# Layer 1's second head in two quarters: turning rows with VectorE and transfers instead of with TensorE

## The chip, the cores and the metric

The kernel runs on one core of a Trainium2 chip. The metric is the time of one execution in microseconds on the device. Lower is better.

## The reference

Four graph layers act on `x` (4096 x 128) with one adjacency matrix `adj` (4096 x 4096). The change lies in layer 1 (two attention heads) and in the preparation of layer 2's input:

```python
# layer 1, for each head i (K = 2)
h = x_norm @ ff0_w[i].T
e = leaky_relu(s_src[:, None] + s_dst[None, :]);  atten = softmax(where(mask, e, NEG), axis=1)
att = _ln(atten @ h + x, g2, b2)
h_next = h_next + elu(att @ ff1_w[i].T) / K
# between the layers
x = x + h_next
h = maximum(_layernorm(x), 0.0)
# layer 2 begins with
Wh = h @ W;  f_src = Wh @ a[:D];  f_dst = Wh @ a[D:]
```

So after a head's sums are complete there are two more small matrix products for each block of rows: `att @ ff1_w.T`, and, after the second head, `h @ W` for the next layer. For either one, the rows have to be turned (features on the partitions).

## The kernel before

The 4096 rows of the result are worked in four quarters (`Q = 4`) of 1024 (`S = 8` blocks of 128), and each quarter is a run over `T = 32` tiles k. In layer 1 (h = 1 and h = 2 for its two heads) VectorE makes for each tile k one tile of exponentials, 128 x 1024, into one of four slots (`ring`, L1323). TensorE multiplies it into `acc` in two halves of 512 columns (L504, two records of the trace for each half, so four for a tile). VectorE can be at most four tiles ahead, because tile k waits until TensorE has used tile k - 4.

There is no planner. Small work is hung behind fixed tiles by lists `ks`: `run(h, q, at(ks, steps))` runs step j on that engine directly after its tile `ks[j]`. TensorE, VectorE and ScalarE work through their programs in order, and talk by semaphores. During run (2, q) the engines finish quarter q - 1 of the second head (`post1(1, q - 1)`), and prepare that quarter's input of layer 2 (`feed(3, ...)`):

- ScalarE copies `acc` to `U` as soon as the previous run has ended (`wide_take`, L978), TensorE turns the sums back (`sums_back`, L557), VectorE divides, adds the residual from `V`, and takes statistics (L1454, L1127 to L1140). Step `scal` (L1146, L1150) gives scale and shift, and ScalarE writes normalised rows to `V` (L788, signal `n_norm`).
- TensorE turns `V` by eight transposes into `turn` (L519), ScalarE widens `turn` into `U` with scale and bias (L810, `n_wide`), TensorE multiplies by `ff1T` (`apply`, L570), ScalarE takes exp and relu (L1017, L1018), VectorE forms the elu and adds to `X` (L1470, L1482, `post_done`).
- VectorE takes statistics of `X`, ScalarE normalises again into `V` (`f_norm`), TensorE turns `V` (L519), ScalarE widens it to `U` with sums in `hpart` (L808, `f_wide`), VectorE adds those sums (`halves`, L1190), TensorE multiplies by `proj2` (`project`, L542), and ScalarE copies the result to `G` and `score2` (L882, L884, `f_placed`).

In TensorE's and ScalarE's programs the runs (2, 1) and (2, 2) are the two turns of a loop whose q is a register; run (2, 3) is written out. In VectorE's all are written out. With q a register, `fixed(q)` is false. At the head of ScalarE's loop stands a load of the activation table (shown at L978).

The first head turns its rows in another way already: VectorE transposes 32 x 32 blocks from `V` to `U` (L1501, `small_turned`), and `move_blocks` (L275) puts the blocks in place by 16 transfers of 32 KB from `U` back to `V`, eight issued from SP's queue and eight from ScalarE's. ScalarE then waits for `blocks_moved` and widens `V` into `U` (L1011).

`bring_back(q)` in SP's queue (L431) loads the saved input of quarter q into `V` for the residual, when `V` has been read.

Of the kernel before, what the change touches and what calls it, by code (L numbers as in the profile page):

```python
# [64 lines left out]
def graph_layers(nc, x, adj, adj_t, diag, alpha, w0_t, bias0, ff0, ff0_t, ff1_t, attn, g1, b1, g2, b2,  # L65
# [17 lines left out]
    EDGE = (2, 3, 0, 1)  # L83
    EB = len(EDGE)
    SPARE = 2
    WEIGHTS = 15
    WARM = 7

    with ExitStack() as ctx:
# [150 lines left out]
        def fixed(v):  # L240
            return isinstance(v, int)
# [22 lines left out]

        flat_v = V[:, :, :].rearrange("p s d -> p (s d)")

        def move_blocks(eng, q, groups):

            eng.wait_ge(small_turned, q + 1)
            given, taker = (U[:, 0:QC], flat_v) if q < Q else (part_turned, U[:, 0:QC])  # L270
            for i in groups:
                for d in range(4):
                    src = given[32 * i:32 * i + 32, :].rearrange("p (s d r) -> p s d r", d=4, r=32)[:, :, d, :]
                    dst = taker[32 * d:32 * d + 32, :].rearrange("p (s i r) -> p s i r", i=4, r=32)[:, :, i, :]
                    eng.dma_start(dst, src).then_inc(blocks_moved, 16)  # L275
# [8 lines left out]
        def all_summed(h, q):  # L284

            n = q + h * Q
            if h in (1, 2):
                return acc_summed[1], n + 1
            return acc_summed[NB - 1], n + 1 if h == 0 else n + 1 - 2 * Q

        def last_of(q):
            return fixed(q) and q == Q - 1
# [45 lines left out]
        def _(sp):  # L338
# [87 lines left out]
            def bring_back(q):  # L426
                if q == 0:
                    sp.wait_ge(post_done, 2 * Q)
                else:
                    sp.wait_ge(f_turned, q + Q + 1)  # L430
                sp.dma_start(V[:, :, :].rearrange("p s d -> p (s d)"), span(inputs1, q * QC, QC)).then_inc(back, 16)  # L431
            sp.wait_ge(*all_summed(1, Q - 1))
            load_rows(2, 2)
# [1 line left out]
            move_blocks(sp, 3, (0, 1))  # L435
            sp.wait_ge(saved, 16 * Q)
            bring_back(0)
            bring_back(1)
            bring_back(2)
            bring_back(3)  # L440

# [37 lines left out]
        def _(pe):  # L479
# [42 lines left out]
            def feed(h, p, weights, wide, spreads, posts):  # L522

                at = p if h == 0 else Q if h == 1 else p - 2 * Q + 1

                def turned():
                    pe.wait_ge(f_norm, p + 1)
                    wait(pe, rows_kept, spreads)
                    if h == 1:
                        for s in range(S):  # L530
                            mm = pe.transpose(turn[:, s * P:(s + 1) * P], G[:, 1, (p - Q) * S + s, 0:P], ident[:, :])
                    else:
                        mm = turn_v()
                    mm.then_inc(f_turned, 1)

                def project():
                    pe.wait_ge(f_wide, at + 1)
                    wait(pe, f_placed, p if h < 3 else p - Q)
                    wait(pe, post_done, posts)
                    for s in range(S):  # L540
                        dst = mix[:, 0, s * 4:s * 4 + 4] if h == 1 else mix[:, s // 3, (s % 3) * PW:(s % 3) * PW + wide]
                        mm = pe.matmul(dst, U[:, s * P:(s + 1) * P], weights, start=True, stop=True, skip_group_check=True)  # L542
                    mm.then_inc(f_projected, 1)
                return turned, project

            def post1(h, q, spreads, feeds):

                j = q + h * Q

                def sums_back():  # L550
                    pe.wait_ge(acc_taken, taken(1 + h, q) + 2)
                    if h == 0 and fixed(q) and q == 0:
                        pe.wait_ge(bias_made, late_top[2])
                    elif h == 1 and fixed(q) and q == Q - 1:
                        pe.wait_ge(bias_made, early_top[3])
                    for s in range(S):
                        mm = pe.matmul(mix[:, s // 3, (s % 3) * DW:(s % 3) * DW + DW], U[:, s * P:(s + 1) * P], back_w[h],  # L557
                                       start=True, stop=True, skip_group_check=True)
                    mm.then_inc(rows_back, 1)

                def turned():
                    pe.wait_ge(n_norm, j + 1)
                    pe.wait_ge(rows_kept, spreads)
                    turn_v().then_inc(n_turned, 1)

                def apply():
                    pe.wait_ge(n_wide, j + 1)
                    pe.wait_ge(f_placed, feeds)
                    for s in range(S):
                        mm = pe.matmul(mixed[:, s * P:(s + 1) * P], U[:, s * P:(s + 1) * P], ff1T[:, h, :],  # L570
                                       start=True, stop=True, skip_group_check=True)
                    mm.then_inc(ff_done, 1)
                return (sums_back, apply) if h == 0 else (sums_back, turned, apply)

            def spread_top(i):
                pe.wait_ge(top_placed, i)
# [127 lines left out]
            def stage2(q):  # L704
                m = kept_rows[1]
                if fixed(q) and q == 0:
                    ks = [0, 23]
                    run(2, q, at(ks, post1(0, Q - 1, m, 2 * Q)))
                    return
                steps = post1(1, q - 1, m, q - 1 + 2 * Q) + feed(3, q - 1 + 3 * Q, proj2, D + 2, m, q + 2 * Q)  # L710
                if last_of(q):
                    ks = [1, 11, 12, 25, 26, 27, 29]
                    run(2, q, at(ks, steps + (lambda: spread_top(early_top[3]), lambda: spread_rows(m))))
                else:
                    ks = [1, 13, 15, 27, 28]
                    run(2, q, at(ks, steps))
            stage2(0)
            pe.wait_ge(qv2_placed, 1)
# [58 lines left out]
        def _(act):  # L777
# [55 lines left out]
            def feed(h, p, q, between=()):  # L833
# [33 lines left out]
                at = p if h == 0 else Q if h == 1 else p - 2 * Q + 1  # L867
                if h == 3:
                    wait(act, half_summed, 0 if fixed(q) and q == 0 else q * 1)
                    widen(f_turned, at + 1, f_wide, halves=True)  # L870
                else:
                    widen(f_turned, at + 1, f_wide)
                for step in between:
# [114 lines left out]
            def post1(h, q, beside=(), fed=False):  # L988
# [14 lines left out]
                    settle()  # L1003
                normalise(of_v, lambda s: U3[:, s, 0:D], local(scale), local(shift), ACT.Identity, n_norm)
                act.wait_ge(n_norm, j + 1)
                if h == 0:
                    move_blocks(act, q, (2, 3))
                    act.wait_ge(blocks_moved, 256 * (q + 1))
                    for c in range(2):
                        half = slice(c * BANK, (c + 1) * BANK)  # L1010
                        ins = act.activation(U[:, half], flat_v[:, half], ACT.Identity, bias=b2c, scale=g2c)  # L1011
                    ins.then_inc(n_wide, 1)
                else:
                    widen(n_turned, q + 1, n_wide, g2c, b2c)
                ready(ACT.Exp)
                act.wait_ge(ff_done, j + 1)
                act.activation(V[:, :, :], mixed3, ACT.Exp)  # L1017
# [79 lines left out]

            def store(q):
                wide_take(q + 4 * Q)
                move_blocks(act, Q + q, range(4))  # L1100
                act.wait_ge(post_done, q + 4 * Q + 1)
                act.dma_start(span(out.rearrange("(t p) d -> p t d", p=P), q * S, S), V[:, :, :]).then_inc(stored, 16)
            for q in range(Q - 1):
# [9 lines left out]
        def _(dve):  # L1113
# [42 lines left out]
            def feed(h, p, q):  # L1156
# [30 lines left out]
                def halves():  # L1187
                    dve.wait_ge(f_wide, p - 2 * Q + 2)
                    wait(dve, half_summed, 0 if fixed(q) and q == 0 else q * 1)
                    dve.scalar_tensor_tensor(hmean, hpart[0], hpart[1], hmean, ALU.add, ALU.add).then_inc(half_summed, 1)  # L1190
                steps = statistics(lambda s: blocks(X, q, 1, s)[:, 0, :], f_var) + [first_scales]
                if h == 1:
                    half, rest = statistics(of_v, f2_var)
# [1 line left out]
                if h == 1 and not (fixed(p) and p == 2 * Q - 1):  # L1195
                    steps += [lambda c=c: dots(c) for c in range(4)]
                if h == 3:
                    steps += [halves]
                return steps

            def of_v(s):
# [233 lines left out]
            def post1(h, q):  # L1435
# [63 lines left out]
                def small_turns():  # L1499
                    dve.wait_ge(n_norm, j + 1)  # L1500
                    dve.transpose(flat, V[:, :, :].rearrange("p s d -> p (s d)")).then_inc(small_turned, 1)  # L1501
                turns = [small_turns] if h == 0 else []
                steps = [residual, residual_rest] + statistics(lambda s: U3[:, s, 0:D], n_var) + [scal] + turns + [elu, add]
                return steps if h == 0 else steps + [own_pattern, own_pattern_rest]

# [33 lines left out]
            def stage2(q):  # L1539
                steps = post1(1, q - 1) + feed(3, q - 1 + 3 * Q, q - 1)  # L1540
                if last_of(q):
                    ks = [4, 4, 6, 8, 10, 17, 17, 12, 14, 19, 21, 24, 28, 29, 30]
                    run(2, q, at(ks, steps + early_of(3)))
                else:
                    ks = [4, 5, 8, 10, 12, 19, 20, 13, 16, 21, 23, 25, 29]
                    run(2, q, at(ks, steps))
            for q in range(1, Q):
                stage2(q)
# [61 lines left out]
            def post3(q):  # L1610
# [23 lines left out]

                def first_half():
                    st.wait()
                    dve.wait_ge(blocks_moved, 256 * (Q + q + 1))
                    if q > 0:
                        dve.wait_ge(stored, q * 16)
                    st.mark(results(slice(0, HALF)))  # L1640
# [48 lines left out]
```

## Time and profile before

| | us |
|---|---|
| time, median of 3 runs | 1198.27 (1197.99 to 1199.12) |
| time of the profiled execution | 1198.28 |
| its span | 1196.5 |
| TensorE busy in the span | 1191.9 |
| VectorE busy | 936.4 |
| ScalarE busy | 301.6 |

The span runs from the first to the last instruction; the profiled execution's time holds 1.8 us more, which lies around it. Busy time counts matmuls until their modelled end, so it doesn't say that TensorE is at its peak. Granted clock is given as a share of 2.4 GHz, and was 1.00 over the span.

### The profile page before, as it was taken

How to read it: one execution, taken by the hardware profiler on the slowest of the kernel's cores; microseconds unless marked ns; L12 is line 12 of the kernel's file. 1: busy time of each engine (PE TensorE's matmuls, PEld its weight loads, DVE VectorE, ACT ScalarE, POOL GpSimd, SP SyncE). 2: the span in 40 equal slices, each digit the busy share in tenths (PEclk: the TensorE clock that was granted, in tenths of full speed). 3: DMA queues.
4: the chain of work that ended last, by engine and by line, in shares of the span. 5: the costliest groups of instructions: out<-in, count | busy, mean ns of one | idle time of the engine just before them, and what ended most of it. 6: DMA issues, size and time to landing. Idle time of an engine off the chain costs nothing.

```text
span 1196.5 us, 16807 instructions
## 1 busy us (share of the span) xinstructions
PE 1191.9 (100%) x6299; PEld 823.5 (69%) x6299; DVE 936.4 (78%) x1704; ACT 301.6 (25%) x732; POOL 10.4 (1%) x21
## 2 busy tenths in 40 slices
PE   9999999999999999999999999999999999999999
PEld 9999999965444444444544547999999974444455
DVE  5548675798878788878888796798787869887886
ACT  3312122234323232422323134541212121000000
POOL 3000000000000000000000000000000000000000
PEclk9999999999999999999999999999999999999999
DMA  9888888700111102110000000022303068999930
GB/s 318 301 270 289 299 293 302 254 23 10 45 18 36 18 35 35 53 18 18 1 18 0 18 1 19 2 86 109 141 0 141 1 258 305 313 332 319 321 85 18
DMA packets 79284, 153.18 MB, mean 128 GB/s; under 512 B 35456, under 2 KB 44016, under 8 KB 79216
## 3 DMA queue, kind: packets, MB, share of 16 engines
q1 hardware_dynamic: 53264, 145.43, 34.8%
q10 hardware_dynamic: 25456, 6.30, 2.4%
q8 instruction: 43, 0.70, 0.2%
q0 software_dynamic: 496, 0.55, 0.1%
q14 instruction: 25, 0.20, 0.1%
HBM read 144.33 MB, written 4.24 MB: 124 GB/s over the span
## 4 chain that ended last, share of the span: by engine, by line
PE 98%; DVE 1%; ACT 0%; issue 0%; DVEq 0%
PE acc L504 51%; PE acc L488 37%; PE acc L761 4%; PE mix L570 1%; PE mix L557 1%; PE mix L542 1%; PE turn L519 1%; PE acc L769 1%; DVE ring L1323 0%; PE turn L515 0%; PE mix L628 0%; PE mix L515 0%; PE turn L638 0%; DVE U L1454 0%; PE mix L645 0%; PE turn L633 0%
## 5 line engine op out<-in xcount | busy, mean ns | idle before, releaser
L1323 DVE SCALAR_TENSOR_TENSOR ring<-G,score,mask 128x1024 f32<-128x1024 f32 x372 | 464.7, 1279 | 62.8 <-PE acc L504 33.0
L504 PE MATMUL acc<-ring,G 128*128 128x512 f32 x1000 | 436.2, 593 | 0.2 <-DVE acc L1263 0.2
L504 PEld LDWEIGHTS acc<-ring,G 128*128 128x128 f32 x1000 | 186.6, 190 | 226.9 <-issue 209.8
L488 PE MATMUL acc<-G,ring 128*128 128x129 f32 x2240 | 254.3, 275 | 0.1
L488 PEld LDWEIGHTS acc<-G,ring 128*128 128x128 f32 x2240 | 252.1, 192 | 1.4 <-issue 1.1
L488 PE MATMUL acc<-G,mask 128*128 128x129 f32 x1648 | 186.2, 275 | 0.0
L488 PEld LDWEIGHTS acc<-G,mask 128*128 128x128 f32 x1648 | 185.0, 192 | 0.0
L504 PE MATMUL acc<-mask,G 128*128 128x512 f32 x384 | 165.8, 593 | 0.0
L1597 DVE TENSOR_TENSOR ring<-ring,mask 128x1024 f32<-128x1024 f32 x120 | 146.7, 1223 | 11.4 <-DVE ring L1597 0.9
L504 PEld LDWEIGHTS acc<-mask,G 128*128 128x128 f32 x384 | 72.6, 190 | 91.0 <-issue 89.8
L1361 DVE TENSOR_SCALAR mask<-mask 128x1024 uint8<-128x1024 f32 x103 | 68.6, 688 | 38.0 <-DMA mask<-in_adj_t 37.7
L800 ACT ACTIVATE dev<-var 128x8 f32<-128x8 f32 x28 | 5.9, 209 | 233.8 <-DVE var L1140 233.8
L978 ACT COPY U<-acc 128x512 f32<-128x512 f32 x22 | 12.9, 585 | 171.1 <-PE acc L504 171.1
L761 PE MATMUL acc<-mask,G 128*128 128x384 f32 (+1 forms) x128 | 48.6, 540 | 0.0
L986 ACT COPY U<-acc 128x387 f32<-128x387 f32 (+1 forms) x24 | 10.4, 446 | 129.2 <-PE acc L488 128.4
L761 PEld LDWEIGHTS acc<-mask,G 128*128 128x128 f32 x128 | 24.2, 190 | 24.0 <-issue 15.6
L788 ACT ACTIVATE V<-X,shift,scale 128x128 f32<-128x128 f32 (+1 forms) x88 | 35.0, 480 | 0.0
L784 ACT ACT_TABLE_LOAD x26 | 33.4, 1283 | 2.7 <-ACT V L788 1.6
L780 ACT COPY cols<-ident 128x1 f32<-128x1 f32 x40 | 7.6, 190 | 90.2 <-DVE shift L1150 29.1
L788 ACT ACTIVATE V<-U,shift,scale 128x128 f32<-128x128 f32 x64 | 25.5, 480 | 8.8 <-DVE shift L1150 8.8
L1177 DVE SCALAR_TENSOR_TENSOR V<-G,ring 128x128 f32<-128x128 f32 x96 | 21.3, 286 | 5.3 <-ACT G L788 5.2
L488 PE MATMUL acc<-G 128*128 128x129 f32 x160 | 19.6, 276 | 0.3 <-DVE G L1323 0.3
(210 smaller groups left out, 692.6 us busy)
## 6 DMA issues: line engine op xcount, KB each, us to landing
mask<-in_adj SPq DMA_DIRECT2D x128, 512.0 KB, 5.5
mask<-in_adj_t SPq DMA_DIRECT2D x103, 512.0 KB, 4.9
ring<-in_adj_t SPq DMA_DIRECT2D x18, 512.0 KB, 4.9
G<-given_rows SPq DMA_DIRECT2D x10, 512.0 KB, 3.9
G<-in_adj_t SPq DMA_DIRECT2D x4, 512.0 KB, 5.1
inputs<-V ACTq DMA_DIRECT2D x4, 512.0 KB, 2.7
V<-inputs SPq DMA_DIRECT2D x4, 512.0 KB, 3.9
X<-in_x SPq DMA_DIRECT2D x3, 512.0 KB, 9.9
```

Of the source, the lines that this page charges most:

```text
L488: mm = pe.matmul(acc[:, b, (s % 3) * DW:(s % 3) * DW + DW], lhs[:, s * P:(s + 1) * P], g, start=(k == 0 and s % 3 == 0), stop=(k == T - 1) ...
L504: mm = pe.matmul(acc[:, c, :], g, moving[:, c * BANK:(c + 1) * BANK], start=(k == 0), stop=(k == T - 1), skip_group_check=True)
L519: mm = pe.transpose(turn[:, s * P:(s + 1) * P], V[:, s, :], ident[:, :])
L542: mm = pe.matmul(dst, U[:, s * P:(s + 1) * P], weights, start=True, stop=True, skip_group_check=True)
L761: mm = pe.matmul(acc[:, c, 0:n], G[:, 0, k, 0:P], stream3[:, k, c * BANK:c * BANK + n], start=(k == 0), stop=(k == T - 1), skip_group_chec ...
L784: act.activation(warm[func], ident[:, 0:1], func)
L788: ins = act.activation(dst(s), src(s), func, bias=add(s), scale=mul(s))
L978: act.copy(U2[:, c, :], acc2[:, c, :]).then_inc(acc_taken, 1)
L1177: ins = dve.scalar_tensor_tensor(V[:, s, :], blocks(G[:, 1, :, :], q, 1, s)[:, 0, 0:D], 1.0, dot_w[c], ALU.mult, ALU.mult, accum_out=block ...
L1323: dve.scalar_tensor_tensor(slots[k % L], late_home[h] if early and k >= EARLY else rows_home[h, q], rank[h][:, k:k + 1], span(mask, (q * T ...
L1361: dve.tensor_scalar(span(mask, (q * T + k) * QC, QC), tile0(q, k), 0.0, None, ALU.is_gt).then_inc(mask_made, 1)
L1597: dve.tensor_tensor(added, stream3[:, 0, :] if k == 1 else added, stream3[:, k, :], ALU.add).then_inc(tile_added, 1)
```

## The change

For the first two quarters of the second head (`MOVED = 2`) TensorE's two turns go, both that of the normalised rows and that of layer 2's input. In their place VectorE transposes 32 x 32 blocks of `V` into `U` (`small_turns`), SP and ScalarE issue eight block transfers each for every turn, and ScalarE widens from `V` instead of `turn`. Four turns are numbered on the same counters as the first head's (4 to 7), and the last layer's follow behind them. `bring_back` waits for `f_wide` instead of `f_turned`. The lists of the two runs move with it: TensorE's from [1, 13, 15, 27, 28] with five steps to [1, 16, 30] with three, VectorE's from 13 entries to 15.

```diff
+    MOVED = 2
-        def move_blocks(eng, q, groups):
+        def move_blocks(eng, q, groups, rows=True):
             eng.wait_ge(small_turned, q + 1)
-            given, taker = (U[:, 0:QC], flat_v) if q < Q else (part_turned, U[:, 0:QC])
+            given, taker = (U[:, 0:QC], flat_v) if rows else (part_turned, U[:, 0:QC])
...
+        def moved(q):
+            return not fixed(q) or q < MOVED
+        def turn_of(h, q):
+            return q if h == 0 else Q + 2 * q
...
@@ SP: bring_back @@
-                    sp.wait_ge(f_turned, q + Q + 1)
+                    sp.wait_ge(f_wide, q + Q + 1)
...
             bring_back(0)
+            move_blocks(sp, Q, (0, 1))
+            move_blocks(sp, Q + 1, (0, 1))
             bring_back(1)
+            move_blocks(sp, Q + 2, (0, 1))
+            move_blocks(sp, Q + 3, (0, 1))
             bring_back(2)
...
@@ TensorE: feed, post1, stage2 @@
-                return turned, project
+                return (project,) if h == 3 and (not fixed(p) or p < 3 * Q + MOVED) else (turned, project)
...
-                return (sums_back, apply) if h == 0 else (sums_back, turned, apply)
+                return (sums_back, apply) if h == 0 or moved(q) else (sums_back, turned, apply)
...
-                    ks = [1, 13, 15, 27, 28]
+                    ks = [1, 16, 30]
...
@@ ScalarE: feed, post1 @@
-                    widen(f_turned, at + 1, f_wide, halves=True)
+                    if moved(q):
+                        act.wait_ge(f_norm, p + 1)
+                        move_blocks(act, turn_of(1, q) + 1, (2, 3))
+                        act.wait_ge(blocks_moved, 256 * (turn_of(1, q) + 2))
+                        for c in range(2):
+                            ins = act.activation(U[:, c * BANK:(c + 1) * BANK], flat_v[:, c * BANK:(c + 1) * BANK], ACT.Identity,
+                                                 accum_out=hpart[c])
+                        ins.then_inc(f_wide, 1)
+                    else:
+                        widen(f_turned, at + 1 - MOVED, f_wide, halves=True)
...
-                if h == 0:
-                    move_blocks(act, q, (2, 3))
-                    act.wait_ge(blocks_moved, 256 * (q + 1))
+                if h == 0 or moved(q):
+                    move_blocks(act, turn_of(h, q), (2, 3))
+                    act.wait_ge(blocks_moved, 256 * (turn_of(h, q) + 1))
...
@@ VectorE: feed, post1, stage2 @@
+                def small_turns():
+                    dve.wait_ge(f_norm, p + 1)
+                    dve.transpose(flat, V[:, :, :].rearrange("p s d -> p (s d)")).then_inc(small_turned, 1)
...
-                    steps += [halves]
+                    steps += [small_turns, halves] if moved(q) else [halves]
...
-                turns = [small_turns] if h == 0 else []
+                turns = [small_turns] if h == 0 or q < MOVED else []
...
-                    ks = [4, 5, 8, 10, 12, 19, 20, 13, 16, 21, 23, 25, 29]
+                    ks = [4, 5, 7, 8, 9, 12, 20, 21, 14, 17, 22, 23, 24, 27, 30]
```

VectorE's steps in the order of the new list are: `residual` 4, `residual_rest` 5, statistics 7 and 8, `scal` 9, `small_turns` 12, `elu` 20, `add` 21, `own_pattern` 14 and 17, the feed's statistics 22 and 23, `first_scales` 24, `small_turns` 27, `halves` 30. TensorE's are `sums_back` 1, `apply` 16, `project` 30.

## Rows read from the trace of the kernel before

**Rows 1.** The chain that ended last, whole span, shares by engine.

```profile
PE 98%; DVE 1%; ACT 0%; issue 0%; DVEq 0%
```

**Rows 2.** Windows of runs (2,1) and (2,2): stretch, length, busy by engine, clock, DMA.

```profile
549.45:611.58 62.13, 62.13 (x194) 31.11 (x193) 51.37 (x87) 19.82 (x42) 0.00 (x0) 1.00 0.03 9
611.58:673.83 62.25, 62.25 (x194) 31.20 (x193) 51.36 (x87) 17.15 (x40) 0.00 (x0) 1.00 0.03 8
```

**Rows 3.** Timeline of TensorE: start, length, engine, line, operation, tiles, count.

```profile
549.45 20.76 PE L504 MATMUL acc<-ring,G 128*128 128x512 f32 x48
570.05 1.04 PE L519 MATMUL turn<-ident,V 128*128 128x128 f32 x8
570.93 3.60 PE L504 MATMUL acc<-ring,G 128*128 128x512 f32 x8
574.36 1.95 PE L570 MATMUL mix<-ff1T,U 128*128 128x128 f32 x16
...
599.34 1.95 PE L542 MATMUL mix<-ring,U 128*128 128x130 f32 x16
601.13 8.83 PE L504 MATMUL acc<-ring,G 128*128 128x512 f32 x20
609.80 1.95 PE L557 MATMUL mix<-ring,U 128*128 128x129 f32 x16
...
663.26 8.95 PE L504 MATMUL acc<-ring,G 128*128 128x512 f32 x20
672.04 1.95 PE L557 MATMUL mix<-ring,U 128*128 128x129 f32 x16
```

**Rows 4.** Timeline of VectorE in run (2,1), idle time before in brackets.

```profile
564.25 0.19 DVE L1146 RECIPROCAL scale<-dev 128x8 f32<-128x8 f32 x1
...
578.32 1.22 DVE L1470 SCALAR_TENSOR_TENSOR V<-V,mix 128x1024 f32<-128x1024 f32 x1 [2.47 <-ACT mix L1018]
...
590.38 0.20 DVE L1146 RECIPROCAL scale<-dev 128x8 f32<-128x8 f32 x1
...
590.69 4.87 DVE L1323 SCALAR_TENSOR_TENSOR ring<-G,score,mask 128x1024 f32<-128x1024 f32 x4
```

**Rows 5.** Timeline of ScalarE from run (2,1) to the head of (2,3).

```profile
578.31 1.28 ACT L784 ACT_TABLE_LOAD   x1
579.60 0.20 ACT L784 ACTIVATE cols<-ident 128x1 f32<-128x1 f32 x1
...
590.93 3.18 ACT L788 ACTIVATE V<-X,shift,scale 128x128 f32 x8
597.82 0.60 ACT L808 ACTIVATE U<-turn 128x512 f32<-128x512 f32 x1 [3.71 <-PE turn L519]
...
598.89 0.20 ACT L808 ACTIVATION_READ_ACCUMULATOR U<-turn 128x1 f32 x1
601.42 0.48 ACT L882 COPY G<-mix 128x384 f32 x1 [2.33 <-PE mix L542]
...
602.78 1.28 ACT L978 ACT_TABLE_LOAD   x1
605.62 0.58 ACT L978 COPY U<-acc 128x512 f32<-128x512 f32 x1 [1.56 <-PE acc L504]
...
667.81 0.58 ACT L978 COPY U<-acc 128x512 f32<-128x512 f32 x1 [2.91 <-PE acc L504]
```

**Rows 6.** Timelines of VectorE, ScalarE, SP: second and third turn of the first head.

```profile
395.60 1.23 DVE L1501 STREAM_TRANSPOSE U<-V 128x1024 f32<-128x1024 f32 x1
...
403.74 1.52 ACT L1011 ACTIVATE U<-V,cols 128x512 f32<-128x512 f32 x2 [11.84 <-DMA V<-U]
...
454.19 1.24 DVE L1501 STREAM_TRANSPOSE U<-V 128x1024 f32<-128x1024 f32 x1
...
456.75 5.23 SPq L275 DMA_DIRECT2D V<-U  x8
...
464.53 1.52 ACT L1011 ACTIVATE U<-V,cols 128x512 f32<-128x512 f32 x2 [14.04 <-DMA V<-U]
```

**Rows 7.** The page's DMA issues: median us from issue to landing at the end.

```profile
V<-inputs SPq DMA_DIRECT2D x4, 512.0 KB, 3.9
```

More of the change, by code:

```diff
@@ L1013, in post1 @@
                 else:
-                    widen(n_turned, q + 1, n_wide, g2c, b2c)
+                    widen(n_turned, q + 1 - MOVED, n_wide, g2c, b2c)
                 ready(ACT.Exp)
@@ L1099, in store @@
                 wide_take(q + 4 * Q)
-                move_blocks(act, Q + q, range(4))
+                move_blocks(act, Q + 2 * MOVED + q, range(4), rows=False)
                 act.wait_ge(post_done, q + 4 * Q + 1)
@@ L1636, in first_half @@
                     st.wait()
-                    dve.wait_ge(blocks_moved, 256 * (Q + q + 1))
+                    dve.wait_ge(blocks_moved, 256 * (Q + 2 * MOVED + q + 1))
                     if q > 0:
```

## The prediction

> **What bounds the kernel now.** I read the chain of waits first: 98% of it is TensorE [rows 1]. So time is gained only where TensorE has less to do, and lost wherever it is made to wait. Then the windows of the two runs that the change touches: TensorE is busy through all 62.13 and 62.25 us, VectorE for 51.4 of them, the transfer engines for 3%, the granted clock is 1.00, i.e. 2.4 GHz [rows 2]. The timelines give the pace: 48 records (12 tiles) from 549.45 to 570.05, 1.717 us a tile; sixteen records of a small product take 601.13 - 599.34 = 1.79 us [rows 3]. VectorE needs 4.87 us for four tiles, 1.20 from start to start [rows 4]. It has room, but it works in order, as do the others, so the question is when each step of the long chain comes, not how busy an engine is.
>
> **What is removed.** Eight transposes hold TensorE from 570.05 to 570.93, 0.88 us, and four such groups go: -3.51 us [rows 3]. The row's 1.04 us is the overlapped length; the next matmul starts after 0.88. The Trainium skill (TensorE: Matmul & The Clock Gate, Part 4: PE-mode transpose) gives about 275 ns for a transpose in one kernel; taken as the price of each of 32 it would be an estimate of 8.8 us of gain and a time near 1192.2, but the row here shows eight in 0.88 us.
>
> **When the first product is ready (`apply`, now behind tile 16).** I follow run (2,1), whose tile 2 starts at 549.45. Without the turn, TensorE reaches `apply` after 15 tiles, at 549.45 + 25.75 = 575.20, where it stood at 574.36 before [rows 3]. On VectorE `scal` stands behind tile 9 instead of 12, three tiles of 1.20 earlier: 564.25 - 3.6 = 560.65 [rows 4]. Shift and the start of ScalarE take 0.4, eight normalisations 3.2 [rows 5], so `n_norm` comes at 564.3. VectorE ends tile 12 at 564.6, so its new transpose (1.24) waits for nothing and ends at 565.9. From the end of such a transpose to ScalarE's widening the trace shows 403.74 - 396.83 = 6.9 us (eight issues on each queue and the landing), and 1.52 for widening [rows 6]: `n_wide` at 574.4. That is 0.8 before TensorE asks for it. The first turn in each quarter is hidden, with little to spare.
>
> **When the second is ready (`project`, now behind tile 30).** `apply` is 0.84 later than before, so is the elu: 578.32 + 0.84 = 579.16. From the elu to `first_scales` it was 590.38 - 578.32 = 12.06 us with six tiles between them [rows 4]; now there are four (21 to 24): 12.06 - 2.4 = 9.66, so 588.8. `f_norm` follows 594.11 - 590.38 = 3.7 later [rows 4, 5], 592.5. VectorE ends tiles 25 to 27 at 592.8, transposes until 594.0; 6.9 for the move gives 600.9. The widening that also sums took 599.09 - 597.82 = 1.27 from `turn` [rows 5]. From `V` it isn't in the trace. The nearest rows are that one and the 1.52 of the other widening from `V` [rows 6], so 1.2 to 1.6, and I take 1.31: `f_wide` at 602.2, and 0.2 until the first matmul, 602.4. TensorE would reach `project` at 575.20 + 1.79 + 14 x 1.717 = 601.03. It waits **1.4 us**, in both quarters: +2.8. VectorE stands at `halves` meanwhile, with tile 30 made and tile 31 not: it starts that at 602.4 and ends at 603.7, before TensorE asks for it at 602.4 + 1.79 = 604.2. At tile 24 it is up to 0.1 late (588.9 against 589.0), which the wait at `project` absorbs. `own_pattern` moves by one tile and is waited for by nobody in this stretch.
>
> **The end of the run.** Here is the wait that I think the list makes. `project` had three tiles behind it, now one. Before TensorE can start tile 0 of the next run, ScalarE has to copy its results (`G`, `score2`) and after that the first half of `acc`. Let s be the start of `project`, 599.34 before. ScalarE's copies are over at 602.76 = s + 3.42, and the load of the activation table at the head of the loop ends at 604.06 = s + 4.72 [rows 5]. Both were hidden: `acc` was complete only at 605.4. Now TensorE wants tile 0 at s + 1.79 + 1.72 = s + 3.51, but the copy of `acc` starts at s + 4.74, takes 0.58, and the first matmul stands 0.17 behind it: s + 5.50, a wait of **1.99 us**. After run (2,2) there is no table load (ScalarE's copy at 667.81 has none before it): s + 3.44 + 0.58 + 0.17 = s + 4.19, **0.68**. From both goes what the boundary costs now: 601.13 to 609.80 holds five tiles (8.58) and 0.09 of waiting, 663.26 to 672.04 has 0.20 [rows 3, 5]. Sum: +1.99 + 0.68 - 0.29 = +2.38.
>
> A load of the table is seen with its next activation right behind it, 578.31 + 1.28 against 579.60 [rows 5]. The Trainium skill (ScalarE: Activation LUTs, What ACT_TABLE_LOAD costs) adds about 1.38 us of drain to each change of the set; an estimate by it would put 1.38 more on the first boundary, 1201.3, and the row speaks against it.
>
> **Queues.** SP's sixteen issues of each quarter wait for the same transposes as ScalarE's; before them stands only `bring_back`, long done. `bring_back` of the next quarter now goes at 602.2 instead of 597.8 and lands some 3.9 later [rows 7], 606.1; the residual needs it behind `sums_back` at about 613. Free. On ScalarE nothing else is queued behind its 5.5 us of issues than the widening that needs them. The last layer's block moves get new numbers only. The steps of run (2,3) and all later ones are unchanged and shift with TensorE.
>
> **Sum.** -3.51 + 2.80 + 2.38 = +1.67 us: run (2,1) becomes 63.7 long, run (2,2) 62.4. The profiled execution has 1198.28 (a span of 1196.5 and 1.8 around it), the median of the runs is 1198.27, so 1199.95; I say 1200.0. The terms have bounds: the move 6.9 to 9.1 (rival 2), the widening 1.2 to 1.6 (twice -0.1 to +0.3), handovers of 0.1 to 0.2 at six places. If the move took 6.0, because nothing else is on the queues (rows 6 have that already, so I don't expect it), 1.8 would come off.
>
> **Rivals.**
> 1. *The chain fits, and the boundary too: 1194.8.* The whole 3.51 stays. It needs `f_wide` 1.4 us earlier in both quarters, and ScalarE's copies not to be on the path. For it: VectorE has 10 us free in each run, and ScalarE 42 [rows 2]. Against: the chain from `apply` to `project` has no idle step in it except the transfers, and the copy of `acc` behind ScalarE's other copies is program order.
> 2. *The transfers are slower: 1205 to 1207, slower than before.* In the third turn of the first head the widening came 464.53 - 455.43 = 9.1 us behind the transpose, 2.2 more, as SP's issues started only at 456.75 [rows 6]. The first move decides from 0.8 us of excess, the second at once: 2.2 - 0.8 + 2.2 = 3.6 for a quarter, 7.2 for both, 1207; if it hits the second move only, 4.4, so 1204.4. Against: there SP had loads of rows ahead, here it has nothing.
> 3. *Only the boundary waits: 1197.2* (-3.51 + 2.38 = -1.13). If `f_wide` comes by 601.0. It would take a shorter move or a quicker VectorE between elu and transpose.
> 4. *The boundary is hidden, `project` waits: 1197.5* (-3.51 + 2.8). It needs ScalarE's table load or copies to have gone elsewhere.
>
> **Chances.** What can be told from no change here is 0.2%, 2.4 us: below 1195.9 is faster, above 1200.7 slower. Forecast 0.60, of which 0.14 lies above 1200.7 (handovers that I put too low add up in one direction, since each is a link of one chain); rival 1 0.13; rival 2 with its smaller forms 0.12; rivals 3 and 4 together 0.15. So faster 0.13, same 0.61, slower 0.26. The range leaves out rival 1 and the worst of rival 2: 1196.4 to 1202.2; the likeliest case alone spans 1199.0 to 1201.4.
>
> **What would show it.** TensorE's timeline without the turns between tiles and `apply` right behind 15 tiles with no gap; a gap of 1.4 us ahead of `project`, released by ScalarE's widening from `V`; one tile, and then gaps of 2.0 and 0.7 ahead of the next run's first matmul, released by ScalarE's copy of `acc`; the two runs 63.7 and 62.4 long. The forecast falls if `f_wide` comes before TensorE has done tile 30, if ScalarE's copy of `acc` begins as soon as `acc` is complete, or if a gap stands ahead of `apply`.

## The result and the profile after

The changed kernel takes 1200.27 us (median of 20 executions), the kernel before 1198.51 (20): ratio 1.0021, 95% interval 1.0015 to 1.0027. By the medians it is slower by 1.76 us, where 1.67 was forecast; that is clear of the scatter, but inside the 2.4 us that the prediction counts as no change. Here and below the ratio lies near that of the means, not of the medians. The means lie 2.5 us apart, because four of the 20 executions took 1203.1 to 1206.9; TensorE's mean granted clock was 0.997 to 0.999 in these four, and 1.000 in the 16 others. Disturbed executions far above all others (3246 and 1374 us of the kernel before, 5276 of experiment 6) don't count in the ratios. The profiled execution has 1199.71 (span 1197.9) against 1198.28. The windows of the two runs answer to [rows 2]:

```profile
549.29:612.93 63.64, 60.88 (x178) 29.45 (x177) 53.17 (x89) 19.85 (x42) 0.00 (x0) 1.00 0.13 25
612.93:675.26 62.33, 60.85 (x178) 29.46 (x177) 53.17 (x89) 17.09 (x40) 0.00 (x0) 1.00 0.13 25
```

The first run is 1.51 us longer than before, the second 0.08, and TensorE's busy time is 1.25 and 1.40 us less: it has less to do and waits more. TensorE's timeline (as [rows 3], with idle time before in brackets) has the waits:

```profile
549.29 25.91 PE L515 MATMUL acc<-ring,G 128*128 128x512 f32 x60
575.05 1.95 PE L581 MATMUL mix<-ff1T,U 128*128 128x128 f32 x16
576.83 24.26 PE L515 MATMUL acc<-ring,G 128*128 128x512 f32 x56
602.14 2.05 PE L553 MATMUL mix<-ring,U 128*128 128x130 f32 x16 [1.05 <-ACT U L886]
604.02 1.88 PE L515 MATMUL acc<-ring,G 128*128 128x512 f32 x4
607.61 3.70 PE L515 MATMUL acc<-ring,G 128*128 128x512 f32 x8 [1.70 <-ACT U L998]
...
665.81 2.05 PE L553 MATMUL mix<-ring,U 128*128 128x130 f32 x16 [1.09 <-ACT U L886]
667.70 1.88 PE L515 MATMUL acc<-ring,G 128*128 128x512 f32 x4
669.97 3.67 PE L515 MATMUL acc<-ring,G 128*128 128x512 f32 x8 [0.39 <-ACT U L998]
```

`apply` (L581) stands right behind 15 tiles. Ahead of `project` (L553) there is a wait released by ScalarE's widening from `V`. One tile follows, and then a wait released by ScalarE's copy of `acc`, long in the first run and short in the second. (Brackets count from the modelled end of the last matmul; from start to start the waits are longer, as used below.) ScalarE's timeline, as [rows 5], has the reason for the last pair:

```profile
600.68 0.63 ACT L886 ACTIVATE U<-V 128x512 f32<-128x512 f32 x1 [8.28 <-DMA V<-U]
...
605.68 1.28 ACT L998 ACT_TABLE_LOAD   x1
606.97 1.07 ACT L998 COPY U<-acc 128x512 f32<-128x512 f32 x2
...
669.16 1.15 ACT L998 COPY U<-acc 128x512 f32<-128x512 f32 x2
```

The chain of waits over the same stretch, pieces in order of time, names the links:

```profile
579.00 1.22 DVE V L1493
...
589.06 3.58 DVE ring L1346 x3
592.64 1.17 DVE U L1213
593.83 0.62 ACTq L276
...
598.72 1.93 DMA V<-U
...
602.14 2.06 PE mix L553 x16
...
605.68 1.28 ACT L998
...
607.61 3.70 PE acc L515 x8
```

### The profile page after: what moved, and what is told of

It reads as the page before. It is cut to its first block, busy times and chain, and to the rows that moved or that the text cites. A ratio compares the mean times of both kernels' runs of the same rounds, so it can differ in the third digit from the quotient of the medians.

```text
span 1197.9 us, 16813 instructions
## 1 busy us (share of the span) xinstructions
PE 1188.8 (99%) x6267; PEld 820.4 (68%) x6267; DVE 939.8 (78%) x1708; ACT 301.5 (25%) x732; POOL 10.4 (1%) x21
## 3 DMA queue, kind: packets, MB, share of 16 engines
HBM read 144.33 MB, written 4.24 MB: 124 GB/s over the span
## 4 chain that ended last, share of the span: by engine, by line
PE 94%; DVE 3%; ACT 1%; ACTq 1%; issue 1%; DMA 0%; DVEq 0%
PE acc L515 46%; PE acc L499 37%; PE acc L772 4%; DVE ring L1346 2%; PE mix L553 1%; PE mix L581 1%; PE mix L568 1%; ACTq L276 1%; PE acc L780 1%; PE turn L530 1%; DMA V<-U 0%; PE turn L526 0%; PE mix L639 0%; DVE X L1505 0%; DVE V L1493 0%
## 5 line engine op out<-in xcount | busy, mean ns | idle before, releaser
L1031 ACT ACTIVATE U<-V,cols 128x512 f32<-128x512 f32 x12 | 9.1, 806 | 67.0 <-DMA V<-U 67.0
```

## The experiments

My theory was that of the prediction: the loss is made by two waits, both of the second turn and the place of `project`. Each kernel has 5 to 12 executions, and is compared with executions of the kernel before that ran beside it (their medians are 1198.3 to 1198.5). The edits are against the changed kernel, and are shown cut.

**1. Rows' turn alone.** The feed's turn goes back to TensorE.

```diff
-                return (project,) if h == 3 and (not fixed(p) or p < 3 * Q + MOVED) else (turned, project)
+                return turned, project
...
-                    ks = [1, 16, 30]
+                    ks = [1, 16, 27, 28]
...
-                    ks = [4, 5, 7, 8, 9, 12, 20, 21, 14, 17, 22, 23, 24, 27, 30]
+                    ks = [4, 5, 7, 8, 9, 12, 20, 21, 14, 17, 22, 23, 24, 29]
```

> Only the rows' turn goes to VectorE and the transfers; layer 2's input is turned by TensorE again, behind tile 27, with project behind 28. My theory (the loss comes from two waits of TensorE, ahead of project and at the end of the run, both made by the second turn and the place of project) expects both gone and two groups of transposes saved: 2 x 0.88 = 1.75 us below before, about 1196.6 against 1198.4, runs (2,1) and (2,2) 61.3 long. The rival, that VectorE's transposes and the block transfers cost TensorE something by themselves wherever they stand, expects about half of the loss of the whole change, +0.9, about 1199.3.

Measured: 1196.81, ratio 0.9987 (0.9978 to 0.9995), 1.7 below before. TensorE's timeline: no wait at `project`, 8.66 us for the five tiles of the run's end.

```profile
595.37 1.04 PE L528 MATMUL turn<-ident,V 128*128 128x128 f32 x8
596.24 1.88 PE L513 MATMUL acc<-ring,G 128*128 128x512 f32 x4
597.96 1.95 PE L551 MATMUL mix<-ring,U 128*128 128x130 f32 x16
599.75 8.83 PE L513 MATMUL acc<-ring,G 128*128 128x512 f32 x20
608.41 1.95 PE L566 MATMUL mix<-ring,U 128*128 128x129 f32 x16
```

Run (2,1) is 610.20 - 548.89 = 61.3 long, as expected. The first turn, made in both quarters, is a plain gain of its two groups of transposes. The rival is out.

**2. The feed's turn alone**, first form. TensorE's list is [1, 13, 15, 30]. VectorE's steps from the elu on stand one tile earlier, so `halves` is behind tile 29, while `project` stays behind 30.

> Only the turn of layer 2's input goes to VectorE and the transfers; the normalised rows are turned by TensorE behind tile 13, apply stands behind 15, project behind 30, VectorE's steps from the elu on one tile earlier. My theory (the loss sits in the second turn and its place): two groups of transposes saved, -1.75; TensorE comes to project 0.5 us after its input is ready, so no wait there; the gaps at the end of 1.96 and 0.65 stay, -0.29 for what stood there before: +0.6, about 1199.1. The rival, that a moved turn costs by itself through VectorE's extra work, expects the same half of the loss in this kernel as in the one with the rows' turn alone, where it was a gain of 1.7: so 1.7 below before.

Measured: 1208.03, ratio 1.0078 (1.0064 to 1.0092), five executions. Neither expectation held. TensorE waited ahead of tile 30 itself:

```profile
604.51 3.41 PE L513 MATMUL acc<-ring,G 128*128 128x512 f32 x4 [3.82 <-DVE ring L1344]
...
672.15 2.79 PE L513 MATMUL acc<-ring,G 128*128 128x512 f32 x4 [2.48 <-DVE ring L1344]
```

The fault is in the list: `halves` waits for `f_wide` and stands ahead of VectorE's tile 30, which TensorE needs before `project`. After the first wait the four records of a tile take 3.2 us (604.51 to 607.72) instead of 1.7, at a mean granted clock of 0.56.

**3. The same with `halves` behind tile 30.** The edit is against experiment 2.

```diff
-                    ks = [4, 5, 7, 8, 9, 19, 20, 14, 17, 21, 22, 23, 26, 29]
+                    ks = [4, 5, 7, 8, 9, 19, 20, 14, 17, 21, 22, 23, 26, 30]
```

> The kernel with the turn of layer 2's input alone, with VectorE's halves behind tile 30 instead of 29. In the first form TensorE stood 3.8 and 2.5 us ahead of tile 30, which VectorE had not made, because halves stood ahead of it and waited for f_wide; then it ran at half clock. My theory: now TensorE gets tile 30 and comes to project when its input is there (0 to 0.7 us of wait), the gaps of 1.96 and 0.65 at the end stay, no half clock: about 0.6 above before, 1199.0 to 1199.7. The rival, that the turn of the input by transfers costs several us in itself, expects 1205 or more again.

Measured: 1200.21, ratio 1.0015 (1.0006 to 1.0024); its profiled execution 1199.02. The place of one tiny step makes 8 us of difference to experiment 2, and the rival is out.

```profile
601.95 1.97 PE L551 MATMUL mix<-ring,U 128*128 128x130 f32 x16
603.75 1.88 PE L513 MATMUL acc<-ring,G 128*128 128x512 f32 x4
607.34 3.70 PE L513 MATMUL acc<-ring,G 128*128 128x512 f32 x8 [1.71 <-ACT U L996]
```

No wait at `project`, the gap at the end as in the changed kernel. The median lies 0.5 above the window expected, which stays unexplained.

**4. No loop head in ScalarE's program.**

```diff
-            quarters(act, 1, Q - 2, lambda q: stage2(q, []))
+            for q in range(1, Q - 1):
+                stage2(q, [])
```

> The changed kernel with ScalarE's runs (2,1) and (2,2) written out in place of the loop, so that no table load stands at the head of the second turn. My theory: the gap at the end of run (2,1) falls from 1.96 to about 0.65 us, as at the end of (2,2); 1.3 us below the changed kernel, about +0.4 against before. The rival that a change of table costs more than its 1.28 us row (a drain of 1.38 behind it) expects 2.7 less, so 1.0 below before; the rival that the gap is not ScalarE's order expects no change against the changed kernel, +1.7.

Measured: 1199.19, 0.7 above before; ratio 1.0015 (1.0006 to 1.0024), higher than the medians give because five of the eleven executions had a lowered clock and took 1201.3 to 1202.9. The profiled one is among these (see the last section). In it no table load stands ahead of the copy of `acc` at the end of run (2,1): the copy at 608.65 waits for `acc` itself. But TensorE is late and slow there, so the size of the gap can't be compared. The six executions with a clock of 1.000 have a median of 1199.03, those of the changed kernel 1200.01 (16) and, in experiment 11, 1200.71 (8): 1.0 to 1.7 less, where 1.3 was expected. This picks executions by their clock after the fact, but both rivals (2.7 less, no change) lie outside it. The changed kernel's own chain above has the load's 1.28 us on the path in run (2,1). The Trainium skill (ScalarE: Activation LUTs, What ACT_TABLE_LOAD costs) counts a drain of about 1.38 us besides; here the copy starts at 606.97, right behind the load (605.68 + 1.28), so the trace doesn't agree.

**5. `project` one tile earlier.** TensorE's list is [1, 16, 29].

> TensorE's list [1, 16, 29]: project one tile earlier, nothing else. My theory: the input of project is ready at the same time, so run (2,1) keeps its 63.6 us (1.7 more wait ahead of project, 1.7 less at the end), and run (2,2) grows by 1.0 to 63.4, because its end needs only 0.65 of cover: +2.7 against before, about 1201.1. The rival, that the change lost because too little stands behind project, expects both gaps at the end to go for no price: 0.7 below before, about 1197.7.

Measured: 1204.35, ratio 1.0053 (1.0040 to 1.0067), five executions, 5.8 above before where my theory had 2.7. The rival is out, but 3 us were not in my account. TensorE's row of `project` in run (2,1), and then windows as [rows 2]:

```profile
603.74 3.83 PE L553 MATMUL mix<-ring,U 128*128 128x130 f32 x16 [4.24 <-ACT U L886]
```

```profile
603.74:607.36 3.62, 3.62 (x16) 3.62 (x17) 3.62 (x4) 0.00 (x0) 0.00 (x0) 0.50 0.48 145
642.75:669.89 27.14, 24.33 (x70) 11.40 (x68) 20.52 (x33) 8.79 (x20) 0.00 (x0) 1.00 0.12 19
669.89:672.86 2.97, 2.97 (x16) 2.97 (x17) 2.97 (x4) 0.00 (x0) 0.00 (x0) 0.62 0.54 170
```

Behind the first wait (4.24) the clock is 0.50, i.e. 1.2 GHz, and the sixteen records take 3.62 us instead of 1.88. From 642.75 to the second wait it is 1.00 again; behind that wait (2.81) it is 0.62 on average, and they take 2.97. The second wait is the 3.0 of my account when counted from start to start (644.54 + 22.32 = 666.86 to 669.89), so what it costs beyond that is the clock's. The wait in run (2,1) was 1.5 us longer than the account, too, as ScalarE's issues of the move took 7.00 us there instead of 5.53.

**6. ScalarE copies `acc` first.**

```diff
+                if take_next:
+                    wide_take(q + 1 + 2 * Q)
                 act.wait_ge(f_projected, at + 1)
...
                     pe.wait_ge(acc_taken, taken(1 + h, q) + 2)
+                    if h == 1:
+                        pe.wait_ge(f_placed, q + 2 * Q)
```

> The changed kernel, but ScalarE copies acc of the run that ends before it copies the results of project (in both moved quarters); sums_back waits for f_placed as mix is shared. My theory: both gaps at the end (1.96 and 0.65) shrink to the 0.1 to 0.2 of before, the waits of 1.28 ahead of project stay: 2.3 us below the changed kernel, 0.6 below before, about 1197.8. Rival: the gap only moves, since sums_back then waits for the copies of project's results behind the table load: no gain against the changed kernel, +1.7.

Measured: 1197.99, ratio 0.9999 (0.9990 to 1.0008), 0.5 below before, 2.3 below the changed kernel, as expected; the rival is out. From `project`'s end three tiles follow without a gap:

```profile
602.26 2.05 PE L553 MATMUL mix<-ring,U 128*128 128x130 f32 x16 [1.51 <-ACT U L888]
604.14 5.40 PE L515 MATMUL acc<-ring,G 128*128 128x512 f32 x12
609.38 1.95 PE L570 MATMUL mix<-ring,U 128*128 128x129 f32 x16
```

This order takes both `project`'s copies and the table load away from in front of the copy of `acc`; it doesn't tell the two apart.

**7. Three queues.** POOL issues four of the sixteen transfers, SP and ScalarE six each.

```diff
...
+            for i in range(2 * MOVED):
+                move_blocks(pool, Q + i, (3,), done=pool_moved)
...
```

> The changed kernel with the 16 transfers of each of the four moved turns on three queues (SP 6, ScalarE 6, POOL 4) instead of 8 and 8. If the length of a move is the time of its issues (0.69 us each on ScalarE), it falls from 6.9 to 5.5 us, the wait ahead of project (1.28) goes in both runs: 2.5 below the changed kernel, 0.8 below before, about 1197.7; the gaps at the end stay. The rival, that POOL's transfers are slower than the two it takes off ScalarE (5.3 to 7.2 us to landing for its loads of weights in the trace of before, against 2.0 for V<-U), expects the move at 8 us or more, a wait of 2.5 or more ahead of project, some lowered clock behind it, and 2 to 5 above the changed kernel.

Measured: 1199.55, ratio 1.0008 (0.9999 to 1.0017), 0.7 below the changed kernel. Neither expectation held: the move is shorter, not longer, but by less than the issues. In run (2,2) it fell from 6.90 to 6.07 us (656.86 + 1.24 to 664.17), not to 5.5, so 0.5 of the 1.3 us at `project` was left (641.12 + 24.03 to 665.63). In run (2,1) ScalarE's six issues took 5.87 us instead of 4.19, and the wait was 1.71. ScalarE has two issues less, 5.53 to 4.19 us, which is 1.34, but the piece of the chain from the last issue's start to the landing grew. First the changed kernel's, then this one's, both of run (2,2):

```profile
662.36 1.97 DMA V<-U
```

```profile
661.68 2.38 DMA V<-U
```

The Trainium skill (DMA: Bandwidth & Descriptors, Rules for kernel authors) says that spreading transfers over more issuing engines saves only their issue time. The trace agrees, and here not even all of the issue time came through: 0.83 of 1.34 us.

**8. No transfers.** The block moves of the four turns are left out, so the rows are not fully turned.

> The changed kernel without the block transfers of the four moved turns (left out, so the rows are not fully turned; VectorE's transposes and ScalarE's widening stay), which takes the 6.9 us of a move out of the chain. My theory: the wait of 1.28 ahead of project is gone in both runs, the gaps of 1.96 and 0.65 at the end stay to 0.1, as they hang on ScalarE's copies and table load: 2.5 below the changed kernel, about 1197.6, clock 1.000 in every execution. The rival that VectorE's lateness, not the move, makes the wait expects project still to be waited for by about 1 us in each run.

Measured: 1197.34, ratio 0.9991 (0.9982 to 1.0000), clock 1.000 in all 11 executions, as expected. `project` isn't waited for, so the rival is out; the end of the run is that of the changed kernel to 0.1 us (606.60 - 601.23 = 5.37 against 5.47):

```profile
577.14 24.26 PE L511 MATMUL acc<-ring,G 128*128 128x512 f32 x56
601.23 1.95 PE L549 MATMUL mix<-ring,U 128*128 128x130 f32 x16
603.02 1.88 PE L511 MATMUL acc<-ring,G 128*128 128x512 f32 x4
606.60 3.70 PE L511 MATMUL acc<-ring,G 128*128 128x512 f32 x8 [1.71 <-ACT U L993]
```

**9. Three queues and `acc` first.**

> Both edits: three queues for the transfers, and ScalarE copies acc before project's results. If the move gets shorter, every wait of TensorE in the two runs is gone and the whole 3.5 us of transposes is gained: about 1195.0. If POOL makes the move longer, it is the kernel with acc first alone (1198.0) plus the longer wait ahead of project, 1200 or more.

Measured: 1196.58, ratio 0.9986 (0.9977 to 0.9995). The profiled execution has 1195.77. In it no gap stands at the runs' ends, and a wait of 0.49 is left at `project` in each of the two runs, 1.0 of the 1.6 us that are missing to 1195.0. The rest is not explained; the executions scatter from 1195.8 to 1198.9.

**10. And the chain one tile earlier.** On top of experiment 9:

```diff
-                    ks = [1, 16, 30]
+                    ks = [1, 15, 30]
...
-                    ks = [4, 5, 7, 8, 9, 12, 20, 21, 14, 17, 22, 23, 24, 27, 30]
+                    ks = [4, 5, 7, 8, 9, 12, 19, 20, 14, 17, 21, 22, 23, 26, 30]
```

> Three queues and acc first, and the chain one tile earlier: TensorE's list [1, 15, 30], VectorE's steps from the elu on one tile earlier, halves still behind tile 30. My theory: apply asks 0.2 us before n_wide at most, project's input is 1.2 us early, no gap at the end, so runs (2,1) and (2,2) take 60.5 each and nearly all of the 3.5 us of transposes is gained: 1195.1. The rival, that VectorE has one tile less in hand and makes TensorE wait for tiles 20 to 24, expects 0.5 to 1.5 us of gaps ahead of L515's tiles there and no more than the 1196.6 of the kernel with both edits.

Measured: 1195.27, ratio 0.9975 (0.9965 to 0.9985): 3.05 of the 3.5 us are gained, and it is the fastest of all, with the least scatter (1194.66 to 1195.56). The rival is out, as no gap stands in TensorE's rows. Run (2,1) is 60.55 long:

```profile
549.40 24.20 PE L518 MATMUL acc<-ring,G 128*128 128x512 f32 x56
573.45 2.05 PE L586 MATMUL mix<-ff1T,U 128*128 128x128 f32 x16
575.34 25.97 PE L518 MATMUL acc<-ring,G 128*128 128x512 f32 x60
601.14 1.95 PE L556 MATMUL mix<-ring,U 128*128 128x130 f32 x16
602.93 5.40 PE L518 MATMUL acc<-ring,G 128*128 128x512 f32 x12
608.17 1.95 PE L573 MATMUL mix<-ring,U 128*128 128x129 f32 x16
609.95 24.20 PE L518 MATMUL acc<-ring,G 128*128 128x512 f32 x56
```

Against the changed kernel it gains 5.0 us by the medians, about what leaving out the transfers (2.9) and copying `acc` first (2.3) gain one by one. So the two kinds of wait are nearly the whole loss. That the earlier chain alone, on two queues, would do as well was not tried.

**11. The changed kernel again.**

> The changed kernel again, unchanged, for the spread of its executions. In the profiled one the clock was 1.000 and the second move of run (2,1) took 6.9 us; of its 20 executions four had a mean clock of 0.997 to 0.999 and took 1203 to 1207 us. My theory: in some executions a load of instructions (queue q8) falls beside that move and makes ScalarE's eight issues longer (5.97 to 7.15 us in three kernels that have the same move, 5.5 without); the wait ahead of project is then 1.7 to 3.0 us, and the longest ones leave TensorE at 1.2 GHz for a few us. It expects a median of 1199.5 to 1200.5, some executions at 1202 or more, and those alone with a clock below 1.000; if this profile has a move over 7.2 us, a q8 load beside it. The rival, that the lowered clock comes from the chip and not from the waits, expects executions of the kernel before with a clock below 1.000 as often.

Measured: 1200.96 in ten executions, ratio 1.0025 (1.0016 to 1.0035). Its median lies above the window expected. Two executions were above 1202 (1202.78 and 1203.41), and they alone had a mean clock below 1.000; the 13 of the kernel before had 1.000. In all rounds of these experiments, no undisturbed execution of the kernel before had a lowered clock (0 of 86), nor any of the kernels in whose profile TensorE doesn't wait at `project` (experiments 1, 3, 8 and 10, 0 of 42). It was there in 6 of the changed kernel's 30, in 5 of 11 in experiment 4, in 1 of 11 undisturbed ones in experiment 6, and in all ten of experiments 2 and 5; in experiments 7 and 9, where a part of the wait is left, it was in none of 22. So the lowered clock goes with TensorE's waits, and the rival is out. The load of instructions did not fall inside the move in this profile: it was on its queue at 594.70, ahead of the first issue at 594.84, and the issues took the usual 5.52 us.

## Why the prediction was right

Its steps, with what was measured in the profiled execution:

- *Removal, -3.51*: `apply` comes at 575.05, 25.76 behind tile 2 (25.75 forecast).
- *First turn hidden*: widening starts at 572.52 (572.8 forecast, on a run that starts 0.16 earlier), and nothing waits. Experiment 1 shows it as a plain gain.
- *Wait at `project`, 2 x 1.40*: TensorE would reach it at 576.83 + 24.03 = 600.86 and starts it at 602.14: 1.28, and 1.31 in run (2,2). The transposes began at 592.57 (592.8 forecast) and the move took 6.88 and 6.90. Experiment 8 shows that the move makes the wait.
- *End of run (2,1), 1.99*: 607.61 - 602.14 = 5.47 against 5.50, so 1.96; *(2,2), 0.68*: 4.16 against 4.19, so 0.65. Experiment 6 shows ScalarE's order as the cause, and experiment 4, by medians only, the table load's share.
- *Queues free*: the residual's load went at 602.04 (602.2 forecast), and VectorE's residual of the next run at 613.48 stands right behind its reciprocals, with no wait for the load.

The sum of these is -3.51 + 2.59 + 2.61 - 0.29 = +1.40 against +1.67; the profiled execution came out 1.43 longer. So the mechanism was right term by term, and the difference is nearly all in the wait at `project`, 0.1 less in each run. The medians differ by more, 1.76, which is nearer to the forecast than its terms are; that part is luck. What the prediction lacked is that TensorE's clock can fall behind such waits, as it did in four of the first 20 executions. None of the rivals had this; the upper end of the range, 1202.2, leaves those executions out. The 16 others have a median of 1200.01, 1.50 above before.

One figure of the prediction doesn't come out of its terms. With 8.8 us in place of 3.51 its own sum is -8.8 + 2.80 + 2.38 = -3.62, a time of 1194.7 and not 1192.2. Nothing in the forecast hangs on it, and experiment 1 speaks against the price: two groups of eight transposes were worth 1.7 us, not 4.4.

Experiment 5 shows how close the changed kernel stands to worse: `project` a tile earlier costs 4 us more (1204.35 against 1200.27).

## What to carry to other kernels

Taking work off the bounding engine is worth its time only if what replaces it is a chain that fits between the points where that engine asks. Work the chain out link by link, including the end of the stage, where another engine's program order (here ScalarE's copies and a table load ahead of the copy of `acc`) decides. A step that waits late in one engine's list must stand behind everything that the bounding engine needs before it can release that wait.

## What the runs showed of the hardware

A wait of TensorE can cost more than itself. In the profiles, waits of 1.3 to 2.0 us from start to start left the granted clock at 1.00. Behind those of experiments 2, 4 and 5, of 2.7 to 4.5 us, it was 0.50 for some us, i.e. 1.2 GHz. In experiment 4 the profiled execution waited 2.75 us by its row:

```profile
603.97 2.89 PE L553 MATMUL mix<-ring,U 128*128 128x130 f32 x16 [2.75 <-ACT U L886]
```

```profile
606.00:607.40 1.40, 1.40 (x5) 0.99 (x5) 1.40 (x2) 0.51 (x3) 0.00 (x0) 0.50 0.51 199
```

The clock did not fall in the wait there: in windows of 0.5 us it was 1.00 until 605.0, when TensorE had been at work again for 1 us, 0.50 from 605.5 to 608.0, and 1.00 again from 608.5. In experiment 5 it was 0.50 from the first record behind the wait of run (2,1). No run varies the wait alone, so the length at which the clock falls isn't known from here.

That wait was long because ScalarE's eight issues of the second move took 7.15 us there instead of 5.53, ScalarE's queue in the timeline:

```profile
594.03 7.15 ACTq L276 DMA_DIRECT2D V<-U  x8
```

In run (2,1) that time varied from 5.5 to 7.15 in kernels with the same move, in run (2,2) it was 5.4 to 5.5. The DMA queues of this kernel from 596 to 597 us (packets, MB, share) show a load of instructions:

```profile
q8 instruction: 1, 0.02, 7.6%
```

It stands at 596.30 to 596.35, and the chain of waits shows that the fourth issue, which began just ahead of it, is the long one. First the changed kernel's fourth issue, then this one's:

```profile
596.04 0.65 ACTq L276
```

```profile
596.20 1.76 ACTq L276
```

The other profiles fit. In experiments 5 and 7 the load came at 596.25 and 596.40, and the issue begun at 596.19 or 596.27 took 1.85 or 2.07 us. In experiment 2 it came at 597.30, and the issues took 6.83 in all. Where it came ahead of the first issue (experiments 3, 6 and 11) the eight took 5.88, 5.97 and 5.52, and with none beside the move (the changed kernel's first profile) 5.53. That the load makes the issue wait is the likely reading, but no run moves the load on purpose, so the cause is not shown. How such waits are spread over the executions stays open too, as only one of each kernel is profiled.
